# Head softmax in a megakernel: eight of fourteen products ahead of the first tile, six between half tiles, and GpSimd's clears ahead of the norm

## Chip, cores and metric

The kernel is one program on one core of a Trainium2 chip. The metric is the device time of a launch in microseconds (us), less is better. The core's engines are TensorE (PE in the rows; PEld is its weight load), VectorE (DVE), ScalarE (ACT), GpSimd (POOL) and SyncE (SP, which issues the loads); each works through its own queue in order, and they wait for each other by semaphores.

## What is computed

The reference is a chain of eight layers on x of shape (2, 1024, 128), each with a residual and a layer norm ahead of it: attention, a spiking feed-forward layer, a state-space layer, the feed-forward layer again, linear attention, a mixture of eight experts, the attention below, and the experts again. The change touches the seventh, which is stage 6 when they are counted from 0. Its softmax runs over the 16 heads (axis 1), not over the keys:

```python
x = x + _L1_attn_b_ref(_layernorm(x, axis=-1), w_qkv, b_qkv, w_proj, b_proj)
# in _L1_attn_b_ref: N_HEADS = 16, HEAD_DIM = 8
qkv = x @ w_qkv + b_qkv
q, k, v = (qkv[0], qkv[1], qkv[2])          # (batch, head, token, 8)
dp = jnp.einsum('bhqd,bhkd->bhqk', q, k) * SCALE
attn = jax.nn.softmax(dp, axis=1)
w_avg = jnp.einsum('bhqk,bhkd->bhqd', attn, v)
out = w_avg @ w_proj + b_proj
```

## The kernel before

**Layout.** Tokens are 16 blocks of 128 (8 for each batch item). A tile m is 128 keys by 128 queries of all 16 heads; for each block g of queries the 8 tiles of its keys come one after the other, 128 tiles in all. A tile is worked in two half tiles of 64 queries, numbered j, so that tile m is the half tiles 2m and 2m + 1. The 16 heads lie in four groups x of four.

**A half tile j.** TensorE's `scores(j)` (line 1644, four matmuls of 256 columns) writes q.k of all heads into one of three pairs of PSUM banks. VectorE's `maxima(j)` (line 1849) takes the negated maximum over the heads. TensorE's `subtract(j)` (line 1653, two matmuls) adds it in the same banks. ScalarE takes the exponential of them (line 1779). For each whole tile VectorE sums over the heads (`denominators(m)`, line 1856), ScalarE inverts the sums by a logarithm and an exponential (`invert`, lines 1758 and 1760), GpSimd multiplies (line 1602), and TensorE multiplies with v (`pv`, line 1676) four tiles later.

**Products ("jobs").** What the tiles read is made by jobs: ("k", b, x, i) makes k of head group x for 512 tokens of batch item b, ("q", c, x) makes q in the same way, ("v", b, i) makes v of 512 tokens for all heads. For each job TensorE's `make` runs matmuls into one PSUM bank: four of 512 columns for k and q (lines 46, 47, 48 for the high and low parts of x and weights, 1627 for the bias), sixteen of 128 columns for v (lines 46 to 48 and 1623). ScalarE's `take` copies the bank out (line 1735, for v line 1731), and VectorE's `stack` writes k or q from the copy and the bank (lines 1834 and 1840). For v, `stack` has no arithmetic: VectorE waits for ScalarE's copy and raises the count of finished jobs, `s6_st`, by hand. `make(n)` waits for the stack of job n - 2, so two jobs are in flight.

**Order before.** `JOBS` lists them. The fourteen of batch item 0 that are needed first (eight k, two v, four q, in this order) have no place in the loop (`at` is None) and are made in a row ahead of the first scores, in banks 0 and 1. The others have a tile number `at` and are made in the `pv` of that tile. ScalarE's `scatter(g)` (line 1744, four copies) places the q of block g in a buffer `q6` that is zero elsewhere; scatter(0) and scatter(1) run ahead of the loop, those of later blocks in it. `scores` waits for the scatter and for the k that it reads.

**Order of each engine in the loop.** TensorE: subtract(j), scores(j+2), then half a pv. ScalarE: exponential j, then at even j an inverse. VectorE: maxima(j), behind each odd j from 3 on one `denominators`, and at places a stack.

**Clears.** GpSimd zeroes or fills six buffers of this stage and counts them in `s6_z`. `s6_clear` does three once stage 5 has finished (lines 1590 to 1592). Then comes GpSimd's part of the norm (`ln_pool`, lines 171 and 172), and then `s6_pool` clears the other three (lines 1596 to 1598): `wp6` (512 words in each partition), `q6` (6144) and `ot6` (1024). TensorE's first product, VectorE's first stack, ScalarE's scatter and the load of the output weights wait for all six. In the norm VectorE normalizes 16 blocks (line 149), TensorE transposes them (line 190), ScalarE copies the high part (line 205) and VectorE subtracts for the low part (line 164). Ahead of the norm VectorE makes the low parts of the weights (line 1806).

## Time and profile before

| | us |
|---|---|
| median of three runs | 2423.21 |
| lowest and highest | 2420.97, 2427.17 |
| profiled execution, its own time | 2421.62 |
| its span, first to last instruction | 2419.9 |
| norm of stage 6, first of line 149 to first product | 1418.45 to 1432.31 |
| fourteen products and two scatters, to the first maximum | 1432.31 to 1469.11 |
| first six half tiles, to the seventh maximum | 1469.11 to 1481.24 |
| the rest of stage 6's loop | 1481.24 to about 2083 |

A row of a timeline has the start and the length in us, the engine, the line, the operation, what it writes and reads by the program's names with partitions and elements, how many such instructions are merged in the row, and in brackets how long the engine was idle ahead of it and what ended that. A row of windows has for each engine its busy time and instructions, then the clock granted to TensorE as a share of 2.4 GHz (0.50 is 1.2 GHz), the share of the DMA engines and GB/s. ps is PSUM; AF and AR are the two large buffers from which most tensors are cut.

### The profile page before, as it was taken

The page shows a single profiled execution, that of the slowest core. Times are in us where ns is not written, and L with a number is a line of the kernel's source. Part 1 is how long each engine was busy: PE and PEld are TensorE (multiplying, and loading weights), DVE is VectorE, ACT ScalarE, POOL GpSimd, SP SyncE. Part 2 cuts the span into 40 slices and gives each one's busy share as a digit, 9 for nine tenths or more (in the row PEclk, how much of TensorE's full clock was granted, in tenths as well). Part 3 has the DMA queues.
Part 4 walks back from the last instruction along what each step waited for, and adds up shares of the span by engine and source line. Part 5 has one row for each costly group of instructions (what it writes and reads, how often), then busy time and mean ns, then how long its engine had stood idle before and what let it go on. Part 6 is the DMA issues. An engine that isn't in the chain of part 4 may idle for free.

```text
span 2419.9 us, 32295 instructions
## 1 busy us (share of the span) xinstructions
PE 1926.3 (80%) x12320; PEld 1227.9 (51%) x12320; DVE 1694.2 (70%) x2179; ACT 1114.3 (46%) x1839; POOL 972.4 (40%) x366
## 2 busy tenths in 40 slices
PE   6989998655687685577999947788878777499998
PEld 4444443342343343455777734455555545377776
DVE  5656565255794796626666657998999999666666
ACT  2345444313422421114555525666676776355554
POOL 2566777202462363100000024776787888500000
PEclk8899998876898897768999967998999999799999
DMA  2021111000000000001000000000000000100000
GB/s 72 22 54 28 28 27 28 9 10 0 0 0 0 0 1 9 5 9 44 27 27 0 1 5 1 1 2 1 1 1 2 1 2 2 40 27 14 27 1 18
DMA packets 30543, 33.09 MB, mean 14 GB/s; under 512 B 5107, under 2 KB 19190, under 8 KB 30390
## 3 DMA queue, kind: packets, MB, share of 16 engines
q1 hardware_dynamic: 29862, 29.97, 4.8%
q8 instruction: 99, 1.62, 0.3%
q10 hardware_dynamic: 528, 1.05, 0.2%
q14 instruction: 54, 0.44, 0.1%
HBM read 17.12 MB, written 1.05 MB: 8 GB/s over the span
## 4 chain that ended last, share of the span: by engine, by line
PE 43%; issue 19%; DVE 17%; POOL 12%; ACT 5%; DMA 2%; SPq 1%; POOLq 0%; DVEq 0%; ACTq 0%; PEldq 0%
PE ps L46 9%; PE ps L48 7%; PE ps L47 7%; DVE negm L1849 5%; POOL AF L635 4%; POOL hc L1128 3%; POOL AF L1128 3%; PE ps L439 2%; PE ps L423 2%; PE ps L464 2%; PE ps L1676 2%; PE ps L1653 1%; PE ps L1644 1%; POOL AF L1602 1%; PE ps L804 1%
## 5 line engine op out<-in xcount | busy, mean ns | idle before, releaser
L1849 DVE TENSOR_REDUCE negm<-ps 128x64 bf16<-128x1024 f32 x256 | 302.0, 1216 | 29.3 <-PE ps L1644 29.3
L996 DVE TENSOR_TENSOR AF<-ps,AF 128x512 f32<-128x512 f32 x256 | 177.0, 691 | 187.7 <-ACT AF L954 187.5
L635 POOL TENSOR_TENSOR AF<-AF 128x2048 f32<-128x2048 f32 (+3 forms) x73 | 234.3, 3210 | 154.3 <-ACT AF L575 148.3
L46 PE MATMUL ps<-XH,AR 128*128 128x512 f32 x616 | 262.0, 425 | 37.6 <-DVE AF L844 18.3
L1602 POOL TENSOR_TENSOR AF<-AF 128x2048 f32<-128x2048 f32 x64 | 243.8, 3811 | 95.4 <-ACT AF L1760 94.9
L954 ACT ACTIVATE AF<-ps 128x512 f32<-128x512 f32 x256 | 152.9, 597 | 270.2 <-PE ps L48 270.2
L1779 ACT ACTIVATE AF<-ps 128x1024 f32<-128x1024 f32 x192 | 196.9, 1026 | 137.1 <-PE ps L1653 135.1
L48 PE MATMUL ps<-XH,AR 128*128 128x512 f32 x616 | 251.2, 408 | 0.0
L47 PE MATMUL ps<-XL,AR 128*128 128x512 f32 x616 | 250.8, 407 | 0.0
L1644 PE MATMUL ps<-AR 128*128 128x256 f32 x1024 | 216.8, 336 | 16.2 <-ACT AF L1779 11.9
L1653 PE MATMUL ps<-negm,ident_bf 128*128 128x512 bf16 x512 | 161.0, 397 | 82.6 <-DVE negm L1849 82.6
L575 ACT ACTIVATE AF<-ps 128x512 f32<-128x512 f32 (+1 forms) x304 | 155.5, 576 | 148.0 <-PE ps L426 86.5
L1856 DVE TENSOR_REDUCE AF<-AF 128x128 f32<-128x2048 f32 x96 | 218.6, 2277 | 0.0
L1644 PEld LDWEIGHTS ps<-AR 128*128 128x128 f32 x1024 | 162.9, 198 | 64.9 <-ACT AF L1779 24.3
L977 DVE TENSOR_TENSOR AR<-AF,AR 128x512 fp32r<-128x512 f32 x256 | 174.5, 682 | 0.2
L46 PEld LDWEIGHTS ps<-XH,AR 128*128 128x128 f32 x616 | 120.5, 196 | 83.6 <-DVE AF L844 24.6
L964 ACT ACTIVATE AR<-AF 128x512 fp32r<-128x512 f32 x256 | 159.8, 624 | 0.5 <-DVE AF L996 0.5
L1351 DVE TENSOR_TENSOR_SCAN AF<-ps,AF 128x1024 f32<-128x1024 f32 x64 | 146.6, 2291 | 2.2
L1128 POOL TENSOR_TENSOR hc<-AF 128x1024 f32<-128x1024 f32 x32 | 76.5, 2392 | 167.4 <-DVE AF L1351 167.4
L1295 ACT ACTIVATE ps<-ps,AF 128x1024 f32<-128x1024 f32 x64 | 69.6, 1088 | 153.4 <-PE ps L1188 153.3
L705 DVE TENSOR_REDUCE AF<-ps 128x1 f32<-128x384 f32 (+3 forms) x176 | 103.5, 637 | 47.0 <-PE ps L467 46.6
L48 PEld LDWEIGHTS ps<-XH,AR 128*128 128x128 f32 x616 | 120.8, 196 | 29.9
(281 smaller groups left out, 3938.5 us busy)
## 6 DMA issues: line engine op xcount, KB each, us to landing
AR<-AR SPq DMA_DIRECT2D x96, 128.0 KB, 2.4
AF<-in_L_ffn_Wg_dram SPq DMA_DIRECT2D x16, 256.0 KB, 2.8
AF<-in_L_ffn_Wu_dram SPq DMA_DIRECT2D x16, 256.0 KB, 3.1
AF<-in_L_ffn_Wd_dram SPq DMA_DIRECT2D x16, 256.0 KB, 3.7
out_dram<-X SPq DMA_DIRECT2D x1, 1024.0 KB, 5.1
AF<-in_L_attn_a_Wq_dram SPq DMA_DIRECT2D x1, 512.0 KB, 3.6
AF<-in_L_attn_a_Wout_dram SPq DMA_DIRECT2D x1, 512.0 KB, 8.6
AR<-AR SPq DMA_DIRECT2D x32, 8.0 KB, 1.8
```

The costliest lines, as they stand in the source:

```text
L46: pe.matmul(out, ah, bh, start=start, stop=False)
L47: pe.matmul(out, ah, bl, start=False, stop=False)
L48: return pe.matmul(out, al, bh, start=False, stop=stop)
L635: pool.tensor_tensor(zacc[u % 2][:, :, c0:512], zacc[u % 2][:, :, c0:512], pt[t % 4][:, :, 0:w], ALU.add).then_inc(s0_zp, 1)
L996: dve.tensor_tensor(mh[:, m % 3, :], bank(3 + m % 3), msg[:, m % 3, :], ALU.mult).then_inc(m_h, 1)
L1128: pool.tensor_tensor(hcs[u % 4], hs[:, u % 2, :], cc, ALU.mult).then_inc(s2_hc, 1)
L1602: pool.tensor_tensor(p6[m % 3].rearrange("p (j q i) -> p j q i", j=HJ, i=2), e6[m % 4].rearrange("p (j q i) -> p j q i", j=HJ, i=2), w6i[: ...
L1644: ins = pe.matmul(bank(2 * (j % 3) + x // 2)[:, 256 * (x % 2):256 * (x % 2) + 256], k6[:, x, k0:k0 + P], q[:, :, q0:q0 + 2 * SUB], start=x ...
L1653: ins = pe.matmul(bank(2 * (j % 3) + h).rearrange("p (j q i) -> p j q i", j=4, i=2), ident_bf[:, :], negm6[:, j % 4, :].unsqueeze(1).unsqu ...
L1779: act.activation(o[:, :, q0:q0 + 2 * SUB], bank(2 * (j % 3), 2).rearrange("p (j c) -> p j c", j=HJ), ACT.Exp).then_inc(s6_e, 1)
L1849: dve.tensor_reduce(negm6[:, j % 4, :], bank(2 * (j % 3), 2).rearrange("p (j q i) -> p q j i", j=HJ, i=2), mybir.AxisListType.XY, ALU.max, ...
L1856: dve.tensor_reduce(z6[:, m % 2, :], e6[m % 4].rearrange("p (j q i) -> p q j i", j=HJ, i=2), mybir.AxisListType.XY, ALU.add).then_inc(s6_z ...
```

## The change

Only stage 6 is changed. The list `FIRST` holds the jobs made ahead of the first scores: four q and the four k of the first 512 keys. The other four k and the two v are the list `EARLY`: job `EARLY[j]` is made behind `scores(j+2)` on TensorE, copied behind exponential j on ScalarE and stacked behind `maxima(j)` on VectorE, for j from 0 to 5, in banks 6 and 7. `scores(8)`, the first to read the later keys, waits for their k. scatter(1) moves from ahead of the loop to behind exponential 6. GpSimd's three later clears move from behind its part of the norm into `s6_clear`, ahead of it.

```diff
--- before.py
+++ after.py
@@ -1558,11 +1558,14 @@
         def q_jobs(c):
             return [("q", c, x) for x in range(SS)]
 
-        JOBS = [(job, None) for job in kv_jobs(0) + q_jobs(0)]
+        FIRST = q_jobs(0) + [("k", 0, x, 0) for x in range(SS)]
+        EARLY = [("k", 0, x, 1) for x in range(SS)] + [("v", 0, i) for i in range(2)]
+        JOBS = [(job, None) for job in FIRST + EARLY]
         JOBS += [(job, LB * (n // 3) + 2 * (n % 3) + 2) for n, job in enumerate(q_jobs(1) + kv_jobs(1) + q_jobs(2))]
         JOBS += [(job, LB * (8 + n // 3) + 2 * (n % 3) + 2) for n, job in enumerate(q_jobs(3))]
         JOBS = [(n, job, at) for n, (job, at) in enumerate(JOBS)]
-        FIRST_JOBS = [j for j in JOBS if j[2] is None]
+        FIRST_JOBS = JOBS[:len(FIRST)]
+        EARLY_AT = {j: JOBS[len(FIRST) + j] for j in range(len(EARLY))}
         JOBS_AT = {at: (n, job) for n, job, at in JOBS if at is not None}
         MADE = {job: n for n, job, _ in JOBS}
         SCATTER_AT = {LB * (g - 2) + 5: g for g in range(2, NB)}
@@ -1572,7 +1575,9 @@
             return sum(1 for _, _, at in JOBS if at is None or at < t)
 
         def job_bank(n, at):
-            return bank(n % 2) if at is None else bank(6 + (at // LB + 1) % 2)
+            if at is None:
+                return bank(n % 2 if n < len(FIRST) else 6 + n % 2)
+            return bank(6 + (at // LB + 1) % 2)
 
         def s6_load(q, s):
             q.wait_ge(x_done, X_AFTER[s])
@@ -1590,12 +1595,11 @@
             pool.memset(f32(b6), 0.0).then_inc(s6_z, 1)
             pool.memset(f32(bv6), 0.0).then_inc(s6_z, 1)
             pool.memset(f32(ones6), 1.0).then_inc(s6_z, 1)
-
-        def s6_pool(pool, link, s):
-            pool.wait_ge(x_done, X_AFTER[s])
             pool.memset(wp6, 0.0).then_inc(s6_z, 1)
             pool.memset(q6.rearrange("p a b -> p (a b)").bitcast(F32), 0.0).then_inc(s6_z, 1)
             pool.memset(ot6, 0.0).then_inc(s6_z, 1)
+
+        def s6_pool(pool, link, s):
             for m in range(NTI):
                 pool.wait_ge(s6_wi, m + 1)
                 wait(pool, s6_pv, m - 2)
@@ -1635,7 +1639,9 @@
                 if j % (2 * LB) == 0:
                     pe.wait_ge(s6_sc, g + 1)
                     if g % LB == 0:
-                        pe.wait_ge(s6_st, MADE[("k", g // LB, SS - 1, 1)] + 1)
+                        pe.wait_ge(s6_st, MADE[("k", g // LB, SS - 1, 1 if g else 0)] + 1)
+                if j == LB:
+                    pe.wait_ge(s6_st, MADE[("k", 0, SS - 1, 1)] + 1)
                 wait(pe, s6_e, j - 2)
                 k0 = L * (g // LB) + P * kb
                 for x in range(SS):
@@ -1694,6 +1700,8 @@
                 subtract(j)
                 if j + 2 < 2 * NTI:
                     scores(j + 2)
+                if j in EARLY_AT:
+                    make(*EARLY_AT[j])
                 if j // 2 >= LAG:
                     pv(j // 2 - LAG, j % 2)
             for m in range(NTI - LAG, NTI):
@@ -1749,7 +1757,6 @@
                 take(n, job, at)
             act.wait_ge(s6_z, 6)
             scatter(0)
-            scatter(1)
 
             def invert(m):
 
@@ -1778,6 +1785,10 @@
                 q0 = 2 * SUB * (j % 2)
                 act.activation(o[:, :, q0:q0 + 2 * SUB], bank(2 * (j % 3), 2).rearrange("p (j c) -> p j c", j=HJ),
                                ACT.Exp).then_inc(s6_e, 1)
+                if j in EARLY_AT:
+                    take(*EARLY_AT[j])
+                if j == len(EARLY):
+                    scatter(1)
                 if j % 2 == 0 and j >= 4:
                     invert(j // 2 - 2)
                 m = j // 2 - LAG
@@ -1862,6 +1873,8 @@
 
             for j in range(2 * NTI):
                 maxima(j)
+                if j in EARLY_AT:
+                    stack(*EARLY_AT[j])
                 if j % 2 and j >= 3:
                     denominators(j // 2 - 1)
                     m = j // 2 - LAG - 1
```

On VectorE, from the first stack on, this stood before (L1834 and L1840 are stacks, L1849 maxima, L1856 denominators; s6_hi counts ScalarE's copies, s6_s scores, s6_e exponentials):

```order
L1834 SCALAR_TENSOR_TENSOR AR<-AF,ps 128x512 [waits s6_hi,s6_z]
L1834 SCALAR_TENSOR_TENSOR AR<-AF,ps 128x512 [waits s6_hi] x7
L1840 SCALAR_TENSOR_TENSOR AF<-AF,ps 128x512 [waits s6_hi,s6_st]
L1840 SCALAR_TENSOR_TENSOR AF<-AF,ps 128x512 [waits s6_hi] x3
L1849 TENSOR_REDUCE negm<-ps 128x64 [waits s6_s] x4
L1856 TENSOR_REDUCE AF<-AF 128x128 [waits s6_e]
L1849 TENSOR_REDUCE negm<-ps 128x64 [waits s6_sub,s6_s] x2
L1856 TENSOR_REDUCE AF<-AF 128x128 [waits s6_e]
L1849 TENSOR_REDUCE negm<-ps 128x64 [waits s6_sub,s6_s] x2
L1856 TENSOR_REDUCE AF<-AF 128x128 [waits s6_wi,s6_e]
```

and this stands there now, from the second q on (L1845 and L1851 are the stacks, L1860 the maxima, L1867 the denominators):

```order
L1851 SCALAR_TENSOR_TENSOR AF<-AF,ps 128x512 [waits s6_hi] x3
L1845 SCALAR_TENSOR_TENSOR AR<-AF,ps 128x512 [waits s6_hi] x4
L1860 TENSOR_REDUCE negm<-ps 128x64 [waits s6_s]
L1845 SCALAR_TENSOR_TENSOR AR<-AF,ps 128x512 [waits s6_hi]
L1860 TENSOR_REDUCE negm<-ps 128x64 [waits s6_s]
L1845 SCALAR_TENSOR_TENSOR AR<-AF,ps 128x512 [waits s6_hi]
L1860 TENSOR_REDUCE negm<-ps 128x64 [waits s6_s]
L1845 SCALAR_TENSOR_TENSOR AR<-AF,ps 128x512 [waits s6_hi]
L1860 TENSOR_REDUCE negm<-ps 128x64 [waits s6_s]
L1845 SCALAR_TENSOR_TENSOR AR<-AF,ps 128x512 [waits s6_hi]
L1867 TENSOR_REDUCE AF<-AF 128x128 [waits s6_e]
L1860 TENSOR_REDUCE negm<-ps 128x64 [waits s6_sub,s6_s]
```

The last six jobs' stacks have moved behind one maximum each; the two of v show only as waits for s6_hi.

On TensorE, from the end of the last product ahead of the tiles, this stood before (L1627 is the bias of a product, L1644 scores, L1653 subtract):

```order
L1627 MATMUL ps<-one,AR 128x512
L1644 MATMUL ps<-AR 128x256 [waits s6_st,s6_sc,s6_wp]
L1644 MATMUL ps<-AR 128x256 x7
L1653 MATMUL ps<-negm,ident_bf 128x512 [waits s6_max]
L1653 MATMUL ps<-negm,ident_bf 128x512
L1644 MATMUL ps<-AR 128x256 x4
L1653 MATMUL ps<-negm,ident_bf 128x512 [waits s6_max]
L1653 MATMUL ps<-negm,ident_bf 128x512
L1644 MATMUL ps<-AR 128x256 [waits s6_e]
```

and this stands there now (L1631, L1650 and L1659 are the same three):

```order
L1631 MATMUL ps<-one,AR 128x512
L1650 MATMUL ps<-AR 128x256 [waits s6_st,s6_sc,s6_wp]
L1650 MATMUL ps<-AR 128x256 x7
L1659 MATMUL ps<-negm,ident_bf 128x512 [waits s6_max]
L1659 MATMUL ps<-negm,ident_bf 128x512
L1650 MATMUL ps<-AR 128x256 x4
L46 MATMUL ps<-XH,AR 128x512 [waits s6_st]
L47 MATMUL ps<-XL,AR 128x512
L48 MATMUL ps<-XH,AR 128x512
L1631 MATMUL ps<-one,AR 128x512
L1659 MATMUL ps<-negm,ident_bf 128x512 [waits s6_max]
L1659 MATMUL ps<-negm,ident_bf 128x512
```

A product has moved behind the scores of each half tile, ahead of the next subtract.

On GpSimd, from the end of stage 5 to the first multiplication, this stood before:

```order
L1590 MEMSET AR 128x1024 [waits x_done]
L1591 MEMSET one 128x128
L1592 MEMSET one 128x512
L171 TENSOR_SCALAR var_eps<-mv 128x8 [waits ln_stat]
L172 TENSOR_TENSOR rstd<-var_eps,half_pow 128x8 [waits chain_pool]
L171 TENSOR_SCALAR var_eps<-mv 128x8 [waits ln_stat]
L172 TENSOR_TENSOR rstd<-var_eps,half_pow 128x8 [waits chain_pool]
L1596 MEMSET AF 128x512 [waits x_done]
L1597 MEMSET AR 128x6144
L1598 MEMSET AF 128x1024
```

and this stands there now:

```order
L1595 MEMSET AR 128x1024 [waits x_done]
L1596 MEMSET one 128x128
L1597 MEMSET one 128x512
L1598 MEMSET AF 128x512
L1599 MEMSET AR 128x6144
L1600 MEMSET AF 128x1024
L171 TENSOR_SCALAR var_eps<-mv 128x8 [waits ln_stat]
L172 TENSOR_TENSOR rstd<-var_eps,half_pow 128x8 [waits chain_pool]
L171 TENSOR_SCALAR var_eps<-mv 128x8 [waits ln_stat]
L172 TENSOR_TENSOR rstd<-var_eps,half_pow 128x8 [waits chain_pool]
```

The three clears L1596 to L1598 have moved ahead of the norm's four instructions, where they are L1598 to L1600.

## Rows read from the trace of the kernel before

**Rows 1.** The page's head: span and instructions.

```profile
span 2419.9 us, 32295 instructions
```

**Rows 2.** Windows of the head softmax: products, first tiles, loop.

```profile
1432.00:1468.00 36.00, 30.93 (x81) 17.74 (x81) 9.14 (x13) 11.19 (x19) 0.00 (x0) 0.64 0.00 1
1468.00:1481.20 13.20, 10.27 (x44) 6.71 (x44) 11.24 (x8) 9.01 (x12) 0.72 (x1) 0.76 0.00 0
1481.20:2083.00 601.80, 483.99 (x5754) 314.41 (x5754) 577.08 (x412) 401.59 (x641) 486.09 (x126) 0.95 0.01 1
```

**Rows 3.** Line 149 (norm, VectorE): source view; timeline, this and next stage.

```profile
L149 DVE TENSOR_SCALAR R<-X,mv,rstd x128: 328/341/5319, 14.2 to 2116.4; 128x128 f32<-128x128 f32 x128
...
1418.45 9.66 DVE L149 TENSOR_SCALAR R<-X,mv,rstd 128x128 f32<-128x128 f32 x16
...
2112.35 4.36 DVE L149 TENSOR_SCALAR R<-X,mv,rstd 128x128 f32<-128x128 f32 x16
```

**Rows 4.** Timeline: GpSimd's last clear ahead, VectorE's subtractions, GpSimd's long clear.

```profile
1401.82 0.53 POOL L1592 MEMSET one<- 128x512 f32 x1
...
1407.77 5.06 DVE L1806 TENSOR_TENSOR AR<-AF,AR 128x128 fp32r<-128x128 f32 x16 [7.04 <-ACTq L1724]
...
1421.02 5.41 POOL L1597 MEMSET AR<- 128x6144 f32 x1
```

**Rows 5.** Timeline: products, ScalarE's copies and a stack, 1432 to 1455 us.

```profile
1432.31 0.76 PE L46 MATMUL ps<-XH,AR 128*128 128x512 f32 x1 [1.50 <-DVE XL L164]
...
1434.69 0.60 ACT L1735 ACTIVATE AF<-ps 128x512 fp32r<-128x512 f32 x1 [3.25 <-PE ps L1627]
...
1440.43 0.50 PE L46 MATMUL ps<-XH,AR 128*128 128x512 f32 x1 [0.15 <-DVE AR L1834]
...
1441.86 0.60 ACT L1735 ACTIVATE AF<-ps 128x512 fp32r<-128x512 f32 x1 [0.95 <-PE ps L1627]
...
1442.49 0.75 DVE L1834 SCALAR_TENSOR_TENSOR AR<-AF,ps 128x512 fp32r<-128x512 f32 x1 [0.80 <-ACT AF L1735]
...
1446.05 0.60 ACT L1735 ACTIVATE AF<-ps 128x512 fp32r<-128x512 f32 x1 [0.72 <-PE ps L1627]
...
1446.16 0.33 PE L46 MATMUL ps<-AR,XH 128*128 128x128 f32 x1 [0.15 <-DVE AR L1834]
...
1449.48 0.60 ACT L1731 ACTIVATE AF<-ps 128x512 f32<-128x512 f32 x1 [2.83 <-PE ps L1623]
...
1454.41 0.60 ACT L1731 ACTIVATE AF<-ps 128x512 f32<-128x512 f32 x1 [4.34 <-PE ps L1623]
```

**Rows 6.** Timeline: scatters and the first half tiles, to the seventh maximum.

```profile
1465.09 5.44 ACT L1744 ACTIVATE AR<-AF 32x512 fp32r<-32x512 f32 x8 [0.88 <-DVE AF L1840]
...
1469.11 2.36 DVE L1849 TENSOR_REDUCE negm<-ps 128x64 bf16<-128x1024 f32 x2 [4.12 <-PE ps L1644]
...
1470.39 1.03 PE L1653 MATMUL ps<-negm,ident_bf 128*128 128x512 bf16 x2 [0.47 <-DVE negm L1849]
...
1471.46 1.02 ACT L1779 ACTIVATE AF<-ps 128x1024 f32<-128x1024 f32 x1 [0.93 <-PE ps L1653]
1472.08 0.83 PE L1653 MATMUL ps<-negm,ident_bf 128*128 128x512 bf16 x2
...
1479.04 2.28 DVE L1856 TENSOR_REDUCE AF<-AF 128x128 f32<-128x2048 f32 x1
...
1481.24 2.34 DVE L1849 TENSOR_REDUCE negm<-ps 128x64 bf16<-128x1024 f32 x2
```

**Rows 7.** Timeline: subtract, scores and the next work in the loop, high clock.

```profile
1744.54 0.60 PE L1653 MATMUL ps<-negm,ident_bf 128*128 128x512 bf16 x2
...
1745.54 0.66 PE L1676 MATMUL ps<-AF 128*8 128x128 f32 x16
```

**Rows 8.** Windows, all engines, of ten us among the first tiles.

```profile
1475.00:1480.00 5.00, 2.95 (x15) 1.61 (x14) 5.00 (x4) 2.57 (x4) 0.00 (x0) 0.94 0.00 0
1480.00:1485.00 5.00, 3.49 (x14) 2.43 (x13) 5.00 (x4) 2.67 (x6) 3.81 (x1) 0.50 0.00 0
```

## Prediction

> **What bounds the kernel now.** I first read the page's head for the span, then the table by stretches for the head softmax, then the timelines of its norm, of the products ahead of its first tile and of its first tiles. The profiled execution spans 2419.9 us [rows 1]. In the loop over 128 tiles (from the fourth on, 1481.2 to 2083.0 us) VectorE is busy 577.08 of 601.80 us, so VectorE's queue is the limit there and the loop as a whole slides with its start [rows 2]. Ahead of it VectorE works 9.14 of 36.00 us while TensorE makes products [rows 2]: that stretch is a chain from TensorE over ScalarE to VectorE, and the change acts on it and on the norm in front of it. The question is therefore when VectorE starts the maximum of half tile 6 (1481.24 us now [rows 6]), the first one after all moved products, since from there on the order is as before but for one scatter.
>
> **GpSimd's clears.** In the norm of this stage VectorE's 16 normalizing instructions (line 149) take 9.66 us together; the same 16 in the next stage take 4.36 us. One lasts 5319 ns where the median is 341 [rows 3]. It can only be in this norm's group, and GpSimd clears the 6144 words of the query buffer there, from 1421.02 for 5.41 us [rows 4]. From the end of line 149 (1428.11) to the first product it is 4.20 us [rows 3, 5], so the way behind it has no slack to swallow a gain. The change puts the three clears right behind those that end at 1402.35 us; together they write 7680 words, by the 5.41 us of 6144 an estimated 6.8 us, and so run to about 1409.1, ahead of GpSimd's own part in the norm. So the gain is 9.66 - 4.36 = **5.30 us**. The new place overlaps VectorE's subtractions of line 1806, which start at 1407.77 [rows 4], for up to 1.3 us. If they are held up too, the gain is 4.0 us; at the other end it is 5.3. I take 5.3, because only one instruction in 16 was held in the trace, and none that reads two operands.
> The Trainium skill (SBUF — State Buffer, "Who interferes with whom") says that a `tensor_scalar` in its two-port mode and a GpSimd instruction exclude each other for the whole instruction; the trace agrees, with 5319 ns against 341. The same section says that an instruction with two SBUF inputs is held only by a GpSimd instruction that reads SBUF, which a clear does not; by that the loss at the new place is 0 and not 1.3 us.
>
> **Eight products instead of fourteen.** Now the first product starts at 1432.31, ScalarE copies the eighth at 1446.05 for 0.60 us [rows 5], and the last job's chain leads to the first scatter at 1465.09; half tile 0's maximum starts at 1469.11, 4.02 us after the scatter begins [rows 6]. That is 36.80 us from first product to first maximum. In the new order the first eight are four q and four k, all four matmuls of 512 columns as the first eight now are; ScalarE takes the scatter right behind its eighth copy, since the q are long stacked. New: (1446.05 - 1432.31) + 0.60 + 4.02 = 18.36 us. Gain 36.80 - 18.36 = **18.44 us**. With the norm, the first maximum comes 23.7 us earlier. Moving scatter(1) behind half tile 6 shortens nothing here: ScalarE's second scatter ran beside scores and the first maximum.
>
> **Six products between the half tiles.** Each of half tiles 0 to 5 now holds a job, and its three parts stand in such places that nothing overlaps: VectorE's stack(j) stands between maximum j and maximum j+1, waits for ScalarE's copy, which waits for TensorE's product, which stands behind subtract(j) and scores(j+2), and subtract(j) waits for maximum j. So the time from one maximum to the next is a closed chain:
> - maximum to subtract: 1470.39 - 1469.11 = 1.28 us [rows 6];
> - subtract and scores: 1472.08 - 1470.39 = 1.69 us at 1.2 GHz [rows 6], 1745.54 - 1744.54 = 1.00 us at 2.4 GHz [rows 7];
> - a k product to its copy: 1434.69 - 1432.31 = 2.38 us at the low clock, 1441.86 - 1440.43 = 1.43 us at the high one [rows 5];
> - copy to stack 0.63 us, stack 0.75 us [rows 5].
> A k job's half tile: 1.28 + 1.69 + 2.38 + 0.63 + 0.75 = **6.73 us** at 1.2 GHz, 1.28 + 1.00 + 1.43 + 0.63 + 0.75 = **5.09 us** at 2.4.
> A v job has no stack, but VectorE waits for ScalarE's copy of it all the same (the raising of the count stands in its queue). From one v copy to the next it is 4.93 us at the low clock; the first, mostly at the high clock, took 1449.48 - 1446.16 = 3.32 us [rows 5]. So 1.28 + 1.69 + 4.93 + 0.63 = **8.53 us**, or 1.28 + 1.00 + 3.32 + 0.63 = **6.23 us**.
> Two denominators lie in this stretch (behind stack 3 and stack 5) at 2.20 us from start to the next maximum (1481.24 - 1479.04 [rows 6]): 4.4 us, hidden behind nothing.
> Sum of the six half tiles: low clock 4 x 6.73 + 2 x 8.53 + 4.4 = **48.4 us**; high clock 4 x 5.09 + 2 x 6.23 + 4.4 = **37.2 us**. Before, the same six took 1481.24 - 1469.11 = 12.13 us [rows 6]. So 36.3 us are added at the low clock, 25.1 at the high one.
>
> **Which clock.** From 1475 to 1480 us the granted clock was 0.94 while TensorE had gaps in which it waited for VectorE; the next 5 us ran at 0.50 [rows 8]. In the products it rose, from 2.38 us each to 1.43, after some of them had run with hardly a gap, and it fell in the first v job (3.32 us, then 4.93 [rows 5]). Among the new half tiles TensorE has a gap in each: of 5.09 us at the high clock its own parts are 1.00 + 1.43, of 6.73 us at the low clock 1.69 + 2.38. The first is more of a gap than what stood ahead of the fall, the second still has the dense part of 4 us. So I expect changes to and fro, mostly low, and take three quarters at the low clock for the k jobs, (3 x 6.73 + 5.09) / 4 = 6.32 us each, and both v jobs at the low clock, as the second was. This gives 4 x 6.32 + 2 x 8.53 + 4.4 = 46.7 us, **34.6 us** more than before.
>
> **scatter(1) at half tile 6.** ScalarE's four copies take 5.44 / 2 = 2.7 us [rows 6] between exponential 6 and 7. From the start of maximum 6 VectorE has two maxima, a denominator and two more maxima to do before it needs exponential 7: 2.36 + 2.20 + 2.36 = 6.9 us. ScalarE is done after 1.28 us to the subtract, 1.07 to the exponential, 1.02 of it, 2.7 of scatter, about 0.6 for the two short instructions of the inverse (taken at one copy's length) and 1.02 of exponential 7: 7.7 us [rows 5, 6]. Cost 0.8 us; 0 to 2.7 as bounds.
>
> **Sum.** -5.3 - 18.4 + 34.6 + 0.8 = +11.7 us: 2421.62 + 11.7 = **2433.3 us**. 2421.62 us is the profiled execution in all (1.7 beyond its span), 1.6 below the median of 2423.21; against the median the forecast is +10.1 us or 0.4%. In words: ahead of the tiles the six jobs overlapped over three engines and cost 18.4 us with their scatter, among the half tiles they and what waits behind them add about 35.
>
> **Rivals.**
> 1. The clock stays high among the half tiles. Then 37.2 us: -23.7 + 25.1 + 0.8 = +2.2, **2423.8 us**. For it: 1475 to 1480 us had it at 0.94 with gaps [rows 8]; against: the v jobs. Between this and the forecast every mixture is possible. Chance 0.25.
> 2. Everything low, the eight products too. They then take 8 x 2.38 = 19.0 us rather than 13.74 + 0.60 = 14.3: +4.7; and 48.4 rather than 46.7: +1.7. Together 2433.3 + 6.4 = **2439.7 us**. For it: the second v job ran low although TensorE had no gap [rows 5]; against: it rose within a few products now, from 2.38 to 1.43 us [rows 5]. Chance 0.10.
> 3. Faster: the chain is as worked out, but with the loop shifted, its low-clock stretches fall away. VectorE is idle 601.80 - 577.08 = 24.7 us in the loop, at a mean granted clock of 0.95 [rows 2], so a part of that may be TensorE at the low clock. If half of that idle time went (12.3 us) and the half tiles ran at the high clock, 2423.8 - 12.3 = **2411.5 us**. It decides the sign from the point on at which more than 11.7 us of the 24.7 go, or 2.2 with the high clock. Against it: the order in the loop is unchanged, so its gaps come again. Chance 0.05.
> 4. The diff does less than it says: the clears at the new place hold VectorE's line 1806 for 1.3 us: **2434.6 us**. Chance 0.05, inside the range.
> The forecast with its near mixtures has 0.55.
>
> **Numbers.** About 0.3% (7.3 us) is what a measurement here can tell from no change; the three runs before spread from 2420.97 to 2427.17. Slower by more than that (above 2430.5): the forecast but for its lower tail, rivals 2 and 4: 0.65. Within: rival 1 and that tail: 0.30. Faster: 0.05. The range reaches from rival 1 to just below rival 2: 2423 to 2438.
>
> **What would show it.** Line 149 in this norm at about 4.4 us for 16, the first product at about 1427.0, the first maximum at about 1445.4. Then maxima alone, 5.1 to 6.7 us apart with one stack between, two intervals of 6 to 11 us around the v jobs (the longer ones with a denominator), VectorE waiting for ScalarE's copy in each; half tile 6's maximum at about 1492 (1445.4 + 46.7) against 1481.24 now; from there the loop as before. I am wrong if the six intervals sum to less than 35 us (then a part overlaps that I took as closed), if the first product has not moved by 5 us, or if the loop's own length changes by more than 3 us.

## The result and the profile after

| | median | runs | lowest, highest |
|---|---|---|---|
| before | 2423.21 us | 7 | 2419.89, 2427.17 |
| changed | 2439.66 us | 7 | 2431.87, 2444.35 |

The ratio of the changed kernel to the kernel before is 1.0063 (95% interval 1.0047 to 1.0078): slower, as forecast, but the median stands 1.7 us above the range's upper end (2438 us) and 6.4 above the forecast (2433.3 us). A second series, on the chip of the first experiments, had 2436.69 against 2422.30 us, ratio 1.0051 (1.0032 to 1.0071). The times of the changed kernel are wide apart: 2432 to 2434 us in three of the first seven, 2440 to 2444 in four. The profiled execution, of 2431.87 us, is the lowest of its series, 1.4 us from the forecast. In the series below, three single executions stood far out (2501.38 us in r1, 8338.84 in e1, 4501.19 in e3): the medians count them, the ratios don't.

Its timeline, with the columns of [rows 3 to 6]; the lines of the changed kernel are L149 (norm), L1598 to L1600 (the moved clears), L1743 and L1739 (copies of k or q, and of v), L1752 (scatter), L1845 and L1851 (stacks), L1860 (maxima), L1867 (denominators), L1659 (subtract) and L1650 (scores):

```profile
1402.30 5.22 POOL L1599 MEMSET AR<- 128x6144 f32 x1
...
1407.45 0.95 POOL L1600 MEMSET AF<- 128x1024 f32 x1
1407.46 5.05 DVE L1817 TENSOR_TENSOR AR<-AF,AR 128x128 fp32r<-128x128 f32 x16 [7.20 <-ACTq L1732]
...
1418.14 4.36 DVE L149 TENSOR_SCALAR R<-X,mv,rstd 128x128 f32<-128x128 f32 x16
...
1426.69 0.77 PE L46 MATMUL ps<-XH,AR 128*128 128x512 f32 x1 [1.50 <-DVE XL L164]
...
1441.32 0.60 ACT L1743 ACTIVATE AF<-ps 128x512 fp32r<-128x512 f32 x1 [0.95 <-PE ps L1631]
1441.82 2.68 ACT L1752 ACTIVATE AR<-AF 32x512 fp32r<-32x512 f32 x4
...
1445.36 1.22 DVE L1860 TENSOR_REDUCE negm<-ps 128x64 bf16<-128x1024 f32 x1 [2.66 <-PE ps L1650]
```

The long clear now lies from 1402.30 to 1407.52 us and line 149's 16 instructions take 4.36 us, against 9.66 in [rows 3]. The last clear runs to 1408.40, beside the first 0.95 us of VectorE's subtractions (L1817), which take 5.05 us as in [rows 4] (5.06): nothing is held up at the new place. The long clear itself ends as they start. ScalarE copies the eighth product at 1441.32, scatters at once, and the first maximum stands at 1445.36 us against 1469.11 in [rows 6].

```profile
1457.26 1.22 DVE L1860 TENSOR_REDUCE negm<-ps 128x64 bf16<-128x1024 f32 x1
...
1458.53 0.81 PE L1659 MATMUL ps<-negm,ident_bf 128*128 128x512 bf16 x2 [2.61 <-DVE negm L1860]
...
1458.79 1.41 PE L1650 MATMUL ps<-AR 128*128 128x256 f32 x4
...
1460.00 0.63 PE L46 MATMUL ps<-XH,AR 128*128 128x512 f32 x1
...
1462.24 0.60 ACT L1743 ACTIVATE AF<-ps 128x512 fp32r<-128x512 f32 x1 [1.83 <-PE ps L1631]
1462.87 0.75 DVE L1845 SCALAR_TENSOR_TENSOR AR<-AF,ps 128x512 fp32r<-128x512 f32 x1 [4.39 <-ACT AF L1743]
1463.53 1.22 DVE L1860 TENSOR_REDUCE negm<-ps 128x64 bf16<-128x1024 f32 x1
...
1471.51 1.22 DVE L1860 TENSOR_REDUCE negm<-ps 128x64 bf16<-128x1024 f32 x1
...
1480.18 1.23 DVE L1860 TENSOR_REDUCE negm<-ps 128x64 bf16<-128x1024 f32 x1 [7.46 <-DVEq L1842]
...
1488.80 2.29 DVE L1867 TENSOR_REDUCE AF<-AF 128x128 f32<-128x2048 f32 x1 [7.39 <-DVEq L1842]
1491.00 2.34 DVE L1860 TENSOR_REDUCE negm<-ps 128x64 bf16<-128x1024 f32 x2
...
1498.60 2.29 DVE L1867 TENSOR_REDUCE AF<-XN 128x128 f32<-128x2048 f32 x1 [0.80 <-ACT XN L1786]
```

Half tile 2 is one turn of the chain (1457.26 to 1463.53, 6.27 us): maximum, subtract, scores, product, ScalarE's copy, VectorE's stack, the next maximum. VectorE stands idle for 4.39 us ahead of the stack, where in [rows 6] it went from maximum to maximum. The two half tiles with a v job take 8.67 us (1471.51 to 1480.18) and 10.82 with a denominator (to 1491.00). The last row is the denominator that waits 0.80 us for exponential 7, behind the moved scatter.

The windows, with the columns of [rows 2] (the eight products; the six half tiles; the loop behind):

```profile
1426.00:1442.00 16.00, 14.29 (x32) 7.04 (x32) 5.82 (x9) 4.86 (x9) 0.00 (x0) 0.72 0.00 1
1445.00:1491.00 46.00, 27.75 (x91) 19.34 (x89) 14.36 (x12) 10.36 (x14) 3.81 (x1) 0.61 0.00 0
1491.00:2092.80 601.80, 485.30 (x5754) 314.86 (x5754) 576.52 (x412) 403.96 (x644) 482.49 (x125) 0.95 0.01 1
```

In 46 us of half tiles VectorE works 14.36, at a granted clock of 0.61. The loop behind them is as long and as busy as in [rows 2]: 601.80 us, VectorE 576.52.

### The profile page after: what moved, and what is told of

It reads as the page before. It is cut to its first block and busy times, and to the rows that moved or that the text cites. A ratio compares the mean times of both kernels' runs of the same rounds, so it can differ in the third digit from the quotient of the medians.

```text
span 2430.1 us, 32296 instructions
## 1 busy us (share of the span) xinstructions
PE 1929.4 (79%) x12320; PEld 1231.2 (51%) x12320; DVE 1688.5 (69%) x2179; ACT 1114.1 (46%) x1839; POOL 972.0 (40%) x366
## 5 line engine op out<-in xcount | busy, mean ns | idle before, releaser
L1860 DVE TENSOR_REDUCE negm<-ps 128x64 bf16<-128x1024 f32 x256 | 303.3, 1224 | 34.3 <-PE ps L1650 26.9
L1659 PE MATMUL ps<-negm,ident_bf 128*128 128x512 bf16 x512 | 162.7, 401 | 95.6 <-DVE negm L1860 95.6
L1650 PE MATMUL ps<-AR 128*128 128x256 f32 x1024 | 219.2, 339 | 16.6 <-ACT AF L1786 12.0
L1867 DVE TENSOR_REDUCE AF<-AF 128x128 f32<-128x2048 f32 x96 | 219.4, 2286 | 7.4 <-DVEq L1842 7.4
L1650 PEld LDWEIGHTS ps<-AR 128*128 128x128 f32 x1024 | 164.7, 200 | 65.6 <-ACT AF L1786 22.9
```

What stands on the lines that cost most here:

```text
L1650: ins = pe.matmul(bank(2 * (j % 3) + x // 2)[:, 256 * (x % 2):256 * (x % 2) + 256], k6[:, x, k0:k0 + P], q[:, :, q0:q0 + 2 * SUB], start=x ...
L1659: ins = pe.matmul(bank(2 * (j % 3) + h).rearrange("p (j q i) -> p j q i", j=4, i=2), ident_bf[:, :], negm6[:, j % 4, :].unsqueeze(1).unsqu ...
L1860: dve.tensor_reduce(negm6[:, j % 4, :], bank(2 * (j % 3), 2).rearrange("p (j q i) -> p q j i", j=HJ, i=2), mybir.AxisListType.XY, ALU.max, ...
L1867: dve.tensor_reduce(z6[:, m % 2, :], e6[m % 4].rearrange("p (j q i) -> p q j i", j=HJ, i=2), mybir.AxisListType.XY, ALU.add).then_inc(s6_z ...
```

## The experiments

The table sets the profiles side by side. "Start" is the first of GpSimd's clears, "to product" the time from it to the first product, "to maximum" from there to the first maximum, "six" from there to the seventh, "loop" from there to the start of the last of the 256 maxima. Starts of rows merged in the trace are known to 0.1 us. The instructions ahead of "start" are the same in all, so what differs there comes from the execution and not from the kernel. In "six" of e3, e7 and w2 the second v's wait is missing, as its stack stands behind the seventh maximum; in e4 both v are missing.

| kernel | start | to product | to maximum | six | loop | span |
|---|---|---|---|---|---|---|
| before | 1400.8 | 31.5 | 36.8 | 12.1 | 597.3 | 2419.9 |
| changed | 1400.3 | 26.4 | 18.7 | 45.6 | 597.6 | 2430.1 |
| r1_after_again | 1400.5 | 26.3 | 23.0 | 47.7 | 597.8 | 2437.1 |
| e1_clears_only | 1401.3 | 26.4 | 41.0 | 12.7 | 590.7 | 2413.9 |
| e2_products_only | 1398.7 | 31.7 | 18.2 | 47.1 | 597.9 | 2435.1 |
| e3_again | 1400.5 | 26.1 | 23.0 | 21.3 | 597.0 | 2409.5 |
| e7_stack_one_later | 1398.3 | 26.4 | 23.0 | 23.4 | 592.9 | 2406.1 |
| e7_again | 1406.3 | 26.5 | 22.7 | 23.8 | 594.0 | 2415.1 |
| e5_v_ahead | 1398.5 | 26.4 | 32.9 | 30.5 | 591.6 | 2421.4 |
| e4_spread | 1400.2 | 26.3 | 23.0 | 19.1 | 605.9 | 2416.1 |
| w1_change_warm | 1398.8 | 26.8 | 15.9 | 47.0 | 592.9 | 2423.6 |
| w2_e7_warm | 1407.1 | 27.0 | 15.9 | 23.8 | 594.0 | 2409.6 |
| w3_clears_warm | 1401.3 | 26.8 | 34.0 | 12.4 | 590.6 | 2406.9 |

**The changed kernel once more.**

> The changed kernel unchanged, for a second profile and more times. Theory A (the chain in the half tiles costs what its profile shows, 33.4 us for six half tiles against 23.8 us gained, and what lies beyond is TensorE's clock from run to run): times spread again from about 2432 to 2444 us, and if the profile falls on a long run, the extra time stands in stretches at a granted clock of 0.50, in the eight products (up to +4.7 us), in the six half tiles (up to 48.4 us instead of 45.6) or in the loop (longer than 601.8 us). Theory B (the change adds a fixed cost that the first profile hid): a long run shows the loop or another stage longer at the same clock.

Median 2436.69 us. The profile fell on an execution of 2438.84 us, 7.0 above the first profile.

```profile
1426.00:1442.00 16.00, 15.16 (x27) 7.53 (x27) 5.08 (x7) 3.59 (x6) 0.00 (x0) 0.50 0.00 1
1449.00:1497.50 48.50, 30.26 (x92) 20.75 (x91) 14.35 (x12) 10.37 (x14) 3.81 (x1) 0.50 0.00 0
```

```profile
1429.93 0.75 DVE L1851 SCALAR_TENSOR_TENSOR AF<-AF,ps 128x512 f32<-128x512 f32 x1 [3.24 <-ACT AF L1743]
...
1445.95 0.75 DVE L1845 SCALAR_TENSOR_TENSOR AR<-AF,ps 128x512 fp32r<-128x512 f32 x1 [1.55 <-ACT AF L1743]
1449.83 1.22 DVE L1860 TENSOR_REDUCE negm<-ps 128x64 bf16<-128x1024 f32 x1 [3.13 <-PE ps L1650]
...
1456.33 1.22 DVE L1860 TENSOR_REDUCE negm<-ps 128x64 bf16<-128x1024 f32 x1
...
1497.52 2.35 DVE L1860 TENSOR_REDUCE negm<-ps 128x64 bf16<-128x1024 f32 x2
```

In the first profile the clock of the products' stretch was 0.72; here it is 0.50 throughout, though TensorE was busy 15.16 of 16 us, and 0.50 in the whole stretch of the half tiles. From the first stack to the eighth it is 16.02 us, 2.3 for each product; the first maximum comes 23.0 us behind the first product instead of 18.7; the k half tiles take 6.50 us each. Together 4.3 + 2.1 of the 7.0 us lie here, at the same code. The loop differs by 0.2. So theory A holds, with an unequal share: the clock of the products first. The mean granted clock of each whole execution points the same way for the median: in the first series it was 0.892 in the three of 2432 to 2434 us and 0.885 to 0.887 in the four of 2440 to 2444, and it was 0.888 in this profiled one. None of 2440 us or more was profiled, so what they spend beyond r1's is not known.

**Each part alone.** e1 has the kernel before with this, and e2 the changed kernel without it:

```diff
         def s6_clear(pool):
             ...
             pool.memset(f32(ones6), 1.0).then_inc(s6_z, 1)
+            pool.memset(wp6, 0.0).then_inc(s6_z, 1)
+            pool.memset(q6.rearrange("p a b -> p (a b)").bitcast(F32), 0.0).then_inc(s6_z, 1)
+            pool.memset(ot6, 0.0).then_inc(s6_z, 1)

         def s6_pool(pool, link, s):
-            pool.wait_ge(x_done, X_AFTER[s])
-            pool.memset(wp6, 0.0).then_inc(s6_z, 1)
-            pool.memset(q6.rearrange("p a b -> p (a b)").bitcast(F32), 0.0).then_inc(s6_z, 1)
-            pool.memset(ot6, 0.0).then_inc(s6_z, 1)
```

> The kernel before with GpSimd's three clears ahead of the norm and nothing else. Theory A: -5.3 us, about 2418 us, line 149 at 4.4 us for 16 and the rest of the stage 5.3 us earlier, its length within 3 us of before. Rival (the gain is given back by the clock, since the products and the loop start at another moment): within 2 us of before.

Median 2415.80 us against 2422.30, ratio 0.9960 (0.9944 to 0.9977): 6.5 us less, near the 5.3 forecast. But the profile (VectorE alone) shows that the sum hides larger parts:

```profile
1419.11 4.36 DVE L149 TENSOR_SCALAR R<-X,mv,rstd 128x128 f32<-128x128 f32 x16
...
1468.68 2.36 DVE L1848 TENSOR_REDUCE negm<-ps 128x64 bf16<-128x1024 f32 x2 [4.12 <-PE ps L1643]
```

Its windows, with the columns of [rows 2] (products; the loop behind the seventh maximum):

```profile
1428.00:1446.00 18.00, 18.00 (x32) 8.55 (x31) 5.23 (x7) 4.19 (x7) 0.00 (x0) 0.50 0.00 0
1481.40:2072.00 590.60, 474.96 (x5686) 308.88 (x5686) 571.97 (x409) 398.72 (x635) 482.02 (x125) 0.97 0.01 1
```

The norm gives 5.1 us (31.5 to 26.4 in the table). The eight products ran at the low clock, 2.3 us each, at 0.50 with TensorE busy in all of 18.00 us, and the first maximum came 41.0 us behind the first product, 4.2 more than before; the loop then was 6.5 us shorter, with VectorE as busy as before (572 us from the seventh maximum to the last in both) and idle for 18.6 us instead of 24.7, at a mean clock of 0.97 instead of 0.95. So the rest of the stage wasn't as long as before within 3 us part by part, only in sum: 5.1 - 4.2 - 0.6 + 6.5 = 6.8 less. That the median met the forecast is in part luck, since the clock took 4.2 us in one stretch, which the loop gave back in another.

> The change without the move of the clears: products in FIRST and EARLY, clears behind GpSimd's part of the norm as before. Theory A: +5.3 us over the change, so about 2437 us at the least and 2445 us in the middle; first maximum 18.4 us earlier than before, seventh about 15 us later than before. Rival: the six half tiles are shorter with another start, 37 us rather than 45.6, then about 2430 us.

Median 2438.61 us, ratio 1.0064 (1.0040 to 1.0087). Its 47.1 us of half tiles leave nothing of the rival's 37. Against the changed kernel of the same series it is 1.9 us more, where 5.3 were expected, and it lies 6 us below the expected middle of 2445; the intervals of the two ratios overlap and hold both, so the gain of the clears is seen in the norm's rows here and not in the medians.

**The chain opened.** Is it VectorE's place that closes the chain, or ScalarE's? e3 copies and stacks a job one half tile later, e7 only stacks it later:

```diff
 # ScalarE (e3 alone)
             for j in range(2 * NTI):
-                act.wait_ge(s6_sub, j + 1)
                 ...
+                if j - 1 in EARLY_AT:
+                    take(*EARLY_AT[j - 1])
+                act.wait_ge(s6_sub, j + 1)
                 act.activation(o[:, :, q0:q0 + 2 * SUB], ...
                                ACT.Exp).then_inc(s6_e, 1)
-                if j in EARLY_AT:
-                    take(*EARLY_AT[j])
-                if j == len(EARLY):
+                if j == len(EARLY) + 1:
                     scatter(1)
 # VectorE (e3 and e7)
                 maxima(j)
-                if j in EARLY_AT:
-                    stack(*EARLY_AT[j])
+                if j - 1 in EARLY_AT:
+                    stack(*EARLY_AT[j - 1])
```

> The change, but a job made in half tile j is copied by ScalarE just ahead of exponential j+1 and stacked by VectorE behind maximum j+1 (scatter(1) behind exponential 7). That opens the closed chain: VectorE takes maximum j+1 while TensorE makes the product. Theory A: the six half tiles (to the seventh maximum) take 19 to 30 us, TensorE's own time (subtract, scores and a product, 2.4 to 4.1 us with a k job, 4.3 to 6.6 with a v job), instead of 45.6, so 16 to 27 us less than the change: 2407 to 2422 us. Rival (the jobs among the half tiles cost their own time wherever they are stacked): within 5 us of the change.

Median 2411.18 us, ratio 0.9943 (0.9923 to 0.9963). The rows come from a second series of the same kernel.

> The kernel of e3_one_later once more (copies ahead of exponential j+1, stacks behind maximum j+1), for a profile of an ordinary execution. Theory A: about 2411 us as then; six half tiles in 19 to 30 us, VectorE taking maximum j+1 while TensorE makes product j, VectorE without a wait of 4 us for ScalarE's copy of a k job.

Median 2414.35 us, ratio 0.9965 (0.9949 to 0.9982). The timeline of the engines but for weight loads, from one maximum to the next with a k job:

```profile
1454.84 1.22 DVE L1860 TENSOR_REDUCE negm<-ps 128x64 bf16<-128x1024 f32 x1
1455.15 0.50 PE L1631 MATMUL ps<-one,AR 64*128 64x512 f32 x1
1455.69 0.60 ACT L1743 ACTIVATE AF<-ps 128x512 fp32r<-128x512 f32 x1 [0.58 <-PE ps L1631]
1456.12 0.60 PE L1659 MATMUL ps<-negm,ident_bf 128*128 128x512 bf16 x2 [0.46 <-DVE negm L1860]
1456.33 0.75 DVE L1845 SCALAR_TENSOR_TENSOR AR<-AF,ps 128x512 fp32r<-128x512 f32 x1 [0.27 <-ACT AF L1743]
1456.37 0.83 PE L1650 MATMUL ps<-AR 128*128 128x256 f32 x4
1456.76 1.03 ACT L1788 ACTIVATE AF<-ps 128x1024 f32<-128x1024 f32 x1 [0.47 <-PE ps L1659]
1456.99 1.22 DVE L1860 TENSOR_REDUCE negm<-ps 128x64 bf16<-128x1024 f32 x1
```

Maximum 2 runs while TensorE ends product 1; the copy and the stack of job 1 lie beside subtract 2 and scores 4, and maximum 3 follows after 2.15 us instead of 6.27. The six half tiles take 21.3 us, within the expected 19 to 30, though the products ran low (23.0 us). Behind them VectorE waits once more for the second v, 3.1 us, which the changed kernel's 45.6 us hold already.

> The change with only VectorE's stacks one half tile later (behind maximum j+1); ScalarE's copies stay behind exponential j. Theory A (the closed chain is VectorE's place in it): opening it at VectorE alone gives all of it, within 3 us of e3, about 2411 us. Rival (ScalarE's copy behind its own exponential holds exponential j+1 as much): 5 to 20 us above e3.

> The kernel with VectorE's stacks one half tile later once more, beside the other three. 2412 us again, 10 us below the kernel before; profile: six half tiles 20 to 25 us by whichever clock the products and half tiles fall on.

Medians 2411.97 us (0.9950; 0.9934 to 0.9966) and 2416.07 us (0.9968; 0.9955 to 0.9980). VectorE's rows of the first of the two, from the first maxima to the wait for the second v:

```profile
1447.65 2.36 DVE L1860 TENSOR_REDUCE negm<-ps 128x64 bf16<-128x1024 f32 x2 [3.14 <-PE ps L1650]
...
1471.09 1.21 DVE L1860 TENSOR_REDUCE negm<-ps 128x64 bf16<-128x1024 f32 x1
1475.40 1.23 DVE L1860 TENSOR_REDUCE negm<-ps 128x64 bf16<-128x1024 f32 x1 [3.10 <-DVEq L1842]
```

The medians of e3 and e7 agree within their spread, and the six half tiles take 21.3 and 23.4 to 23.8 us, at a granted clock of 0.82 and 0.72. VectorE's place in the chain was the one that closed it. ScalarE's copy behind its own exponential costs 2.5 us at most, and the clock may account for those. The second was 4 us above the expected 2412; its profile starts the stage at 1406.3 us, 8.0 later than that of the first, and from there to the last maximum the two take 665.7 and 666.9 us.

**The v jobs.** e5 makes the two v ahead of the first tile too:

```diff
-        FIRST = q_jobs(0) + [("k", 0, x, 0) for x in range(SS)]
-        EARLY = [("k", 0, x, 1) for x in range(SS)] + [("v", 0, i) for i in range(2)]
+        FIRST = [("v", 0, i) for i in range(2)] + q_jobs(0) + [("k", 0, x, 0) for x in range(SS)]
+        EARLY = [("k", 0, x, 1) for x in range(SS)]
```

> The change with the two v jobs ahead of the first tile as well (ten products ahead, four k between half tiles 0 to 3, scatter(1) behind exponential 4). Theory A: the v half tiles, 8.7 us each, become plain ones of about 1.2 us each, -15 us, and the two v jobs cost 6 to 10 us ahead: -5 to -9 us against the change, 2428 to 2432 us. Rival (jobs cost the same wherever they stand): within 2 us of the change.

Median 2426.90 us, ratio 1.0011 (0.9992 to 1.0031), 9.8 below the changed kernel's 2436.69 of the series before, so 1.1 us below the expected 2428 to 2432.

```profile
1457.70 1.23 DVE L1860 TENSOR_REDUCE negm<-ps 128x64 bf16<-128x1024 f32 x1 [3.13 <-PE ps L1650]
...
1488.19 2.35 DVE L1860 TENSOR_REDUCE negm<-ps 128x64 bf16<-128x1024 f32 x2
```

The six half tiles take 30.5 us instead of r1's 47.7 (-17.2), and the way to the first maximum 32.9 instead of 23.0 (+9.9): -7.3 us, inside the expected -5 to -9. Its loop is 6.2 us shorter than r1's besides. Of the 17.2 us, 15.0 lie behind the fifth maximum, where the v jobs stood; the other 2.2 lie ahead of it, where the jobs are the same and the granted clock was 0.70 instead of 0.50. So a v job costs 7.5 us inside the chain and 4.9 ahead of it, where both kernels run at 0.50.

e4 opens the chain as e3 does and puts the jobs farther apart:

```diff
-        EARLY_AT = {j: JOBS[len(FIRST) + j] for j in range(len(EARLY))}
+        EARLY_AT = {j: JOBS[len(FIRST) + i] for i, j in enumerate((0, 1, 3, 4, 6, 10))}
...
+                    if m == 4:
+                        wait(pe, s6_st, len(FIRST) + len(EARLY))
                     if kb == 0:
-                        wait(pe, s6_st, jobs_before(m))
+                        wait(pe, s6_st, jobs_before(m) if m else len(FIRST) + len(EARLY) - 1)
```

> As e3, with the six jobs at half tiles 0, 1, 3, 4, 6 and 10 instead of 0 to 5, and the second v awaited only by the products with v of the fifth tile. Theory A with TensorE's own time as the limit of e3: the jobs find gaps that VectorE's denominators leave to TensorE, 3 to 8 us less than e3, 2403 to 2408 us. Rival (VectorE's six stacks and waits are what is left in e3): within 2 us of e3.

Median 2419.03 us, ratio 0.9979 (0.9959 to 0.9998): both expectations missed, it is 5 to 8 us above e3.

```profile
1477.34 2.29 DVE L1869 TENSOR_REDUCE AF<-AF 128x128 f32<-128x2048 f32 x1 [6.33 <-DVEq L1844]
...
1490.80 2.29 DVE L1869 TENSOR_REDUCE AF<-AF 128x128 f32<-128x2048 f32 x1 [4.04 <-DVEq L1844]
```

VectorE waits 6.33 and 4.04 us for the copies of the two v: at neither place is a v job hidden behind one half tile, and at half tile 10 TensorE already has the products with v to make. In its profile the loop is 605.9 us, the longest of all, with both waits in it; from the start of the stage to the last maximum it takes 674.3 us against e3's 667.5. How much of it is the second v's place and how much the clock isn't settled.

**The clock.** The last three kernels add matmuls that nobody reads, so that TensorE works up to the first product:

```diff
         def s6_pe(pe, s):
-            ln_pe(pe, s)
+            def spin(n):
+                for _ in range(n):
+                    pe.matmul(bank(5).rearrange("p (a b) -> p a b", a=4), ident_bf[:, :],
+                              ident_bf[:, :].unsqueeze(1).to_broadcast([P, 4, P]), start=True, stop=True)
+
+            pe.wait_ge(x_done, X_AFTER[s])
+            spin(60)
+            ln_pe(pe, s, spin)          # spin(8) ahead of the norm's third transposes
+            spin(6)
```

> The change with 74 extra matmuls of 512 columns (identity by identity into PSUM bank 5, read by no one): 60 once stage 5 is done, where TensorE waits for the norm, 8 between the norm's two pairs of transposes and 6 behind them. They keep TensorE at work up to the first product. Theory C (what lies beyond the forecast is the granted clock of the eight products, which some executions spend at 0.50 throughout): the eight products run at 1.2 to 1.5 us each, the first maximum stands at about 1442 us against 1445.4 and 1449.8 in the two profiles of the change, and the median is 3 to 8 us below that of the change, about 2430 us. Rival (the clock of the products is not what differs): median within 2 us of 2437 us. The six half tiles stay at 45 to 48 us by either.

Median 2428.70 us, ratio 1.0019 (1.0010 to 1.0028), 8 us below the changed kernel's 2436.69, which is of another series and chip (kernels before: 2423.02 and 2422.30), and the twelve times lie between 2425.34 and 2432.06. TensorE's rows, VectorE's, and a window of the six half tiles with the columns of [rows 2]:

```profile
1398.77 14.81 PE L1616 MATMUL ps<-ident_bf 128*128 128x512 bf16 x60 [0.94 <-DVE X L1010]
...
1425.60 0.47 PE L46 MATMUL ps<-XH,AR 128*128 128x512 f32 x1 [0.37 <-DVE XL L164]
```

```profile
1427.71 0.75 DVE L1861 SCALAR_TENSOR_TENSOR AF<-AF,ps 128x512 f32<-128x512 f32 x1 [2.26 <-ACT AF L1753]
...
1437.63 0.75 DVE L1855 SCALAR_TENSOR_TENSOR AR<-AF,ps 128x512 fp32r<-128x512 f32 x1 [0.58 <-ACT AF L1753]
1441.50 1.23 DVE L1870 TENSOR_REDUCE negm<-ps 128x64 bf16<-128x1024 f32 x1 [3.12 <-PE ps L1660]
...
1488.48 2.35 DVE L1870 TENSOR_REDUCE negm<-ps 128x64 bf16<-128x1024 f32 x2
```

```profile
1441.50:1488.50 47.00, 28.71 (x88) 19.42 (x87) 14.39 (x13) 10.37 (x14) 3.81 (x1) 0.54 0.00 0
```

From the first stack to the eighth it is 9.92 us instead of 16.02; the first maximum stands 15.9 us behind the first product instead of 18.7 or 23.0. The half tiles take 47.0 us all the same: the granted clock there is 0.54. Theory C holds and the rival falls: the products' clock is worth 2.8 us against the first profile and 7.1 against r1's. It isn't all of the gain. The spans of r1's profile and this one differ by 13.5 us, of which almost 5 lie in the loop (597.8 and 592.9 us), and those had not been forecast. The times lie 6.7 us apart, where the changed kernel's lay 12.5 apart in the first series and, but for one, 16.8 in the second; that the products' clock makes most of that spread fits, but isn't shown.

> The same extra matmuls in the kernel with VectorE's stacks one half tile later. Theory C: first maximum 5 to 7 us earlier than its 1447.7, six half tiles 20 to 24 us, median 3 to 8 us below 2412 us, so 2404 to 2409. Rival: within 2 us of it.

Median 2410.77 us, ratio 0.9946 (0.9928 to 0.9964). The first maximum came 6.8 to 7.1 us earlier behind the first product than in e7's profiles, the six half tiles stay at 23.8. The median is 1.8 us above the expected 2404 to 2409. Against e7's 2416.07 in the same series it is 5.3 less; its six times spread from 2404.87 to 2416.90, so the median alone would not show it.

> The same extra matmuls in the kernel with only the clears moved. Its profile had the first eight products at 2.3 us each and yet the first maximum at 1468.7, as the last four then ran at the high clock. Theory C: eight products at the high clock, first maximum 4 to 8 us earlier, median 2408 to 2412 us. Rival (the products' clock evens out over fourteen of them): within 2 us of 2416 us.

Median 2408.13 us, ratio 0.9935 (0.9921 to 0.9949), with its six times between 2406.28 and 2409.40: the lowest of all, 7.7 below e1, in another series. Its windows (eight products, then v):

```profile
1428.00:1442.00 14.00, 13.16 (x45) 7.26 (x46) 5.98 (x8) 4.79 (x8) 0.00 (x0) 1.00 0.01 2
1442.00:1450.00 8.00, 8.00 (x25) 5.69 (x25) 0.00 (x0) 1.19 (x2) 0.00 (x0) 0.52 0.00 0
```

The first maximum comes 34.0 us behind the first product instead of e1's 41.0. The v jobs run at a clock of 0.52 even here.

## Why the prediction missed its range

- **Norm, -5.30 us.** Measured 31.5 to 26.4, -5.2. Right, and so was the free new place, but one ground was misread: not one instruction of line 149 in 16 was held in the trace of before but four, two beside the long clear and two beside the last (a source view in two windows, 1421.3 to 1426.2 and 1426.9 to 1427.4 us):

```profile
L149 DVE TENSOR_SCALAR R<-X,mv,rstd x2: 5129/5224/5319, 1421.2 to 1421.4; 128x128 f32<-128x128 f32 x2
...
L149 DVE TENSOR_SCALAR R<-X,mv,rstd x2: 866/958/1049, 1426.5 to 1426.7; 128x128 f32<-128x128 f32 x2
```

  The rule of the Trainium skill on the shared port (SBUF — State Buffer, "Who interferes with whom") fits these and the new place: each `tensor_scalar` that started beside a clear lasted until the clear ended, and the subtractions with two SBUF inputs beside the last clear took 0.28 to 0.29 us like those behind it. One thing in the traces doesn't follow from the rule: beside GpSimd's own `tensor_tensor` of 128x8 elements (L172, 1.71 us from 1418.61 in the changed kernel) line 149's instructions took 0.34 us as elsewhere.
- **Eight products, -18.44 us.** -18.1 in the first profile, -13.8 in r1. Here the failure lies, in the size of this term. The prediction took the durations of the trace of before, 2.38 us falling to 1.43, for the new list, and gave the case of all products at the low clock (rival 2, +4.7) a chance of 0.10. Of the ten profiles without extra matmuls, seven have it (r1, e1, e3, both e7 and e4, in e7_again until the eighth product, and e5 with its ten products) and three not (before, changed, e2). One profile was read as the rule for a thing that changes from run to run.
- **Six half tiles, +34.6 us.** +33.5 in the first profile, +35.6 in r1. The closed chain was right in each term: 5.71 to 6.50 us for a k job against 5.09 to 6.73, 8.67 for a v against 8.53 at the low clock, 2.2 for a denominator. The clock's guess of 6.32 was between the two profiles' 6.0 and 6.5.
- **scatter(1), +0.8 us.** 0.80 us of idle VectorE, exact.
- **The sum** of +11.7 us was +10.2 by the first profile's span and +17.2 by r1's; rival 2 said +18.1 (2439.7 us), and the median is 2439.66. That the two last agree to the tenth is luck: the one starts from the profiled 2421.62 us, the other is a median of executions between 2432 and 2444. The mechanism and the sign of each part were right, and none of the three signs of being wrong that the prediction named came true in either profile (six half tiles 45.6 and 47.7 us, first product 5.6 and 5.5 us earlier, loop 0.3 and 0.5 us longer). Only the term of the eight products was off by more than 2 us, and only where they ran low (4.6 us in r1): the likelier of two states of the clock was given 1 in 10, and the range was drawn to end just below it. The spread of single times (12 us in the first series, against 7 before) had no term in it either.
- **Rival 3**, a loop with fewer stretches at the low clock, came true in part for e1 and not for the change: e1's loop was 6.5 us shorter with the same code, at 0.97 instead of 0.95; e5, e7 and the kernels with extra matmuls have such loops too. The change's was as long as before in both profiles. What decides between the two isn't settled.

## What to carry to other kernels

Work that is moved in between the steps of a loop adds its whole way to each step if the engine that makes the next step has to wait, in its own queue, for the end of that same work. Here VectorE's stack, one half tile later, turned the changed kernel's +14 us into -7 to -11. Trace the way once around the engines; if it comes back to the start, durations add up. But compare with the simplest kernel too: the clears alone give -6.5 us (e1), and by the medians it isn't shown that moved products add to that even with the chain open (2411.97 and 2416.07 us against 2415.80; with extra matmuls 2410.77 against 2408.13). From the start of the stage to its last maximum the profiles have a few us for them: 665.7 and 666.9 us against 670.8, and 660.7 against 663.9. And where TensorE starts from a wait, price its work at both clocks and let the range hold both: one profile shows one of them.

## What the runs showed of the hardware

- TensorE stayed at the low clock through eight products in a row while the profile showed it busy 15.16 of 16 us (r1) or all of 18.00 (e1), and in the profile of the changed kernel with the same instructions as r1's it rose during the fourth. 60 matmuls in bf16 with the same 512 columns took 14.81 us (w1), 0.25 us each against 0.42 us between two of a product's matmuls at 1.2 GHz (1427.26 to 1427.68 in the first profile), at a granted clock of 0.88. What decides it for the products isn't settled.
- The v jobs (sixteen matmuls of 128 columns) of the first batch item ran at the low clock or fell to it in all profiles, 0.52 in w3 right behind 1.00, but for e4's second one, which stood among the products with v and ran at 0.98.
- Extra matmuls on an idle TensorE cost 0.4 to 0.6 us on the way to the first product (26.8 to 27.0 against 26.4 us) and gave back 7 where the products had run low (23.0 to 15.9 us, 41.0 to 34.0), 2.8 against the first profile.
- Two of VectorE's `tensor_scalar` instructions, otherwise 0.34 us, lasted 5.3 and 5.1 us beside a GpSimd clear of 6144 words; its subtractions of two SBUF tensors kept their 0.28 to 0.29 us beside one of 1024 words. Beside the long clear they were not tried.
